# A transformer block with a mixture of experts: layer norm and gates after all tiles instead of tile by tile, and broadcast copies split over two engines

## What is computed

```python
x = x + layernorm(attention(layernorm(x)))
x = x + layernorm(ffn(layernorm(x)))

# ffn(y)
router = sigmoid(y @ gate_w + gate_b)                 # 16 values a token
values, idx = top_k(router, k=2); values /= sum(values)
out = y + mlp(y, shared) + sum(values * mlp(y, experts[idx]))
# mlp(y, wg, wu, wd) = (silu(y @ wg) * (y @ wu)) @ wd, 1024 -> 512 -> 1024
```

## Time and profile before

| what | us |
|---|---|
| two runs | 5123.9 and 5325.3, median 5224.6 |
| the profiled execution | 5133.07 |
| its span, slowest core (core 6) | 5131.5 |
| its eight cores | 5115.5 to 5131.5 |
| TensorE busy | 3719.8 (72%) |
| VectorE busy | 1558.9 (30%) |
| ScalarE busy | 856.7 (17%) |
| GpSimd busy | 125.4 (2%) |

### The profile page before, as it was taken

How to read it: one execution, slowest core, us unless ns; L and a number is a source line. 1 busy time by engine, 2 the same in 40 slices (tenths; PEclk the granted TensorE clock), 3 DMA queues, 4 the chain that set the end, 5 groups by cost and what they waited for, 6 DMA issues and landing times.

```text
span 5131.5 us, 69222 instructions; the slowest of 8 cores (5115.5 to 5131.5 us)
## 1 busy us (share of the span) xinstructions
PE 3719.8 (72%) x22032; PEld 2020.0 (39%) x22032; DVE 1558.9 (30%) x3716; ACT 856.7 (17%) x2069; POOL 125.4 (2%) x128
## 2 busy tenths in 40 slices
PE   0465454499579849948975984995698499479678
PEld 0232222255335425524542542553354255245445
DVE  0421002422432342243234234224323422432333
ACT  0210000211211221121112112112112111211111
POOL 0000000000000000000000000000000000000000
PEclk9777777799779969968986996997799699689889
DMA  9067777045225405513531550452254045135346
GB/s 181 1 119 160 171 169 192 1 164 210 70 85 215 144 17 188 191 49 116 212 117 42 209 188 6 164 210 70 76 216 152 17 177 194 58 115 205 120 149 229
DMA packets 137919, 688.80 MB, mean 134 GB/s; under 512 B 11744, under 2 KB 46560, under 8 KB 65776
## 3 DMA queue, kind: packets, MB, share of 16 engines
q1 hardware_dynamic: 89792, 621.96, 33.6%
q0 software_dynamic: 47792, 62.43, 8.2%
HBM read 676.51 MB, written 70.25 MB: 146 GB/s over the span
## 4 chain that ended last, share of the span: by engine, by line
PE 62%; DMA 10%; DVE 10%; issue 5%; DVEq 5%; ACT 4%; another core or an unknown queue 2%; POOL 1%; ACTq 0%; SPq 0%; POOLq 0%
PE PSA L834 17%; PE PSA L851 17%; PE PSA L893 16%; PE PSA L444 5%; DMA wu_sb<-ewu 5%; DVEq L89 5%; DMA wd_sb<-ewd 3%; DVE psb L537 2%; PE PSA L652 2%; PE PSA L474 2%; ACT psb L522 2%; DMA scru<-wu_sb 1%; DMA scrd<-wd_sb 1%; DVE ssum L529 1%
## 5 line engine op out<-in xcount | busy, mean ns | idle before, releaser
L834 PE MATMUL PSA<-z_fm,wg_sb 128*128 128x384 f16 (+1 forms) x5984 | 1044.4, 334 | 238.0 <-DMA wu_sb<-ewu 202.3
L862 DVE TENSOR_TENSOR us<-PSA,slabA 128x384 f16<-128x384 f32 (+1 forms) x704 | 384.3, 546 | 2291.6 <-PE PSA L851 2291.6
L893 PE MATMUL PSA<-wd_sb,hs 128*128 128x512 f16 x4352 | 992.3, 386 | 64.2 <-DMA wd_sb<-ewd 64.2
L851 PE MATMUL PSA<-z_fm,wu_sb 128*128 128x384 f16 (+1 forms) x5984 | 978.6, 321 | 2.7 <-DVE us L859 1.3
L834 PEld LDWEIGHTS PSA<-z_fm,wg_sb 128*128 128x128 f16 x5984 | 598.6, 101 | 674.7 <-issue 329.7
L851 PEld LDWEIGHTS PSA<-z_fm,wu_sb 128*128 128x128 f16 x5984 | 578.5, 98 | 374.5 <-issue 20.9
L839 ACT ACTIVATE gs<-PSA 128x384 f16<-128x384 f32 (+1 forms) x748 | 355.4, 480 | 2177.3 <-PE PSA L834 2176.8
L893 PEld LDWEIGHTS PSA<-wd_sb,hs 128*128 128x128 f16 x4352 | 430.7, 99 | 578.8 <-issue 101.5
L550 PE MATMUL PSA<-ids,psb 128*128 128x128 f16 x256 | 41.5, 297 | 350.1 <-DVE psb L537 350.1
L872 DVE TENSOR_TENSOR hs<-gs,us 128x384 f16<-128x384 f16 (+1 forms) x748 | 263.6, 352 | 63.1 <-issue 5.3
L410 PE MATMUL PSA<-ids,z_tm 128*128 128x128 f16 x256 | 29.3, 275 | 326.5 <-DVE z_fm L418 191.2
(11 more groups left out here) (91 smaller groups left out, 1759.7 us busy)
## 6 DMA issues: line engine op xcount, KB each, us to landing
wg_sb<-scrg SPq DMA_DIRECT2D x170, 1024.0 KB, 5.9
wu_sb<-scru SPq DMA_DIRECT2D x170, 1024.0 KB, 9.0
wd_sb<-scrd SPq DMA_DIRECT2D x170, 1024.0 KB, 6.9
scrg<-wg_sb SPq DMA_DIRECT2D x17, 1024.0 KB, 3.9
scru<-wu_sb SPq DMA_DIRECT2D x17, 1024.0 KB, 6.6
scrd<-wd_sb SPq DMA_DIRECT2D x17, 1024.0 KB, 4.5
wg_sb<-ewg POOLq DMA_DIRECT2D x16, 1024.0 KB, 11.5
wu_sb<-ewu POOLq DMA_DIRECT2D x16, 1024.0 KB, 15.8
```

Of the source, the lines that this page charges most:

```text
L834: last = e.matmul(PS[:, b, 0:ST], wg_sb[:, wb_i, kc, 128 * i:128 * i + 128], z1_fm[:, kc, 0:ST], start=(kc == 0), stop=(kc == 7))
L851: last = e.matmul(PS[:, b, 0:ST], wu_sb[:, wb_i, kc, 128 * i:128 * i + 128], z1_fm[:, kc, 0:ST], start=(kc == 0), stop=(kc == 7))
L862: em = k.emit("dve", lambda e, i=i, b=b, hp_=eidx % 2, eidx=eidx, ST=ST: e.tensor_tensor(out=us[:, hp_, i, 0:ST], in0=PS[:, b, 0:ST], in1= ...
L893: last = e.matmul(PS[:, bb, :], hs[:, hp_, i, 128 * tq:128 * tq + 128], wd_sb[:, wb_i, i, 512 * jh:512 * jh + 512], start=(first and i == ...
```

## The change

The three functions `emit_A8`, `emit_B1q` and `emit_gate` and the order written out above go. In their place stand three loops: first the output projection and residual of all tiles, then the second layer norm of all tiles with the helpers that the head uses too (all statistics and applies first, then all transposes and copies), then the gates of all tiles, each of which now waits for the copies of all tiles. The instructions are the same as before. The second edit is in the spreading of the router weights: of the 16 copies to wbc, those with an even number move from ScalarE to VectorE.

```diff
-        def emit_A8(q):
-            nonlocal prev_resadd
+        for q in range(NQ):
             bpair = (6, 7) if q % 2 == 0 else (2, 3)
...
-        def emit_B1q(q):
-            k.emit("dve", lambda e, q=q: e.bn_stats(bnst[:, 0, :], x_tm[:, q, 0:512]),
-                   waits=later(x2_mils[q]), drain_before=True)
...
-            y_evac_by_q[q] = evs
-
-        def emit_gate(q):
+        y_mils = ln_stats_apply(x_tm, z1_tm, x2_mils, 2)
+        yfm_mils, ytr_mils = transpose_tm_to_fm(z1_tm, z1_fm, y_mils, ret_tr=True)
+        yfm_all = later(yfm_mils[-1], *yfm_mils)
+
+        sig_mils = []
+        for q in range(NQ):
             b = 6 + q % 2
-            ws = later(*y_evac_by_q[q]) + bank_write_waits(b) + later(m_gw)
+            ws = yfm_all + bank_write_waits(b) + later(m_gw)
...
-        emit_A8(0)
-        if NQ > 1:
-            emit_A8(1)
-        emit_B1q(0)
-        if NQ > 2:
-            emit_A8(2)
-        if NQ > 1:
-            emit_B1q(1)
-        emit_gate(0)
-        if NQ > 2:
-            emit_B1q(2)
-        if NQ > 1:
-            emit_gate(1)
-        if NQ > 2:
-            emit_gate(2)
-        yfm_all = later(*yfm_mils)
...
-                    em = k.emit("act", lambda e, ei2=ei2, b=b, ST=ST: e.activation(
-                        out=wbc[:, ei2, 0:ST], in_=PS[:, b, 0:ST], func=AF.Identity,
-                        bias=0.0, scale=1.0), waits=later(pm), inc=True)
+                    if ei2 % 2 == 0:
+                        em = k.emit("dve", lambda e, ei2=ei2, b=b, ST=ST: e.tensor_copy(
+                            wbc[:, ei2, 0:ST], PS[:, b, 0:ST]), waits=later(pm), inc=True)
+                    else:
+                        em = k.emit("act", lambda e, ei2=ei2, b=b, ST=ST: e.activation(
+                            out=wbc[:, ei2, 0:ST], in_=PS[:, b, 0:ST], func=AF.Identity,
+                            bias=0.0, scale=1.0), waits=later(pm), inc=True)
```

More of the change, by code:

```diff
@@ L732, in emit_gate @@
-        def emit_gate(q):
+        if attn_only:
+            od = k.emit("sync", lambda e, T0=T0, NQ=NQ: e.dma_start(
+                out=outh[T0:T0 + 128 * NQ, :].rearrange("(q p) d -> p q d", p=128),
+                in_=x_tm[:, 0:NQ, :]), waits=later(*x2_mils), inc=("do", 16))
+            prev_x2_mils = x2_mils
+            prev_ytr = []
+            if sub_i + 1 < len(subs):
+                head_mils = emit_head(sub_i + 1)
+            continue
+        y_mils = ln_stats_apply(x_tm, z1_tm, x2_mils, 2)
@@ L754, in emit_gate @@
                         waits=later(t1), drain_before=True, inc=True)
-            sig_mils[q] = sg
-        emit_A8(0)
-        if NQ > 1:
-            emit_A8(1)
-        emit_B1q(0)
-        if NQ > 2:
-            emit_A8(2)
-        if NQ > 1:
-            emit_B1q(1)
-        emit_gate(0)
-        if NQ > 2:
-            emit_B1q(2)
-        if NQ > 1:
-            emit_gate(1)
-        if NQ > 2:
-            emit_gate(2)
-        yfm_all = later(*yfm_mils)
[L774 to L782, removed]
+            sig_mils.append(sg)
         wsb_mils = []
```

## The result

The changed kernel takes 5040.3 us (median of 11 executions, the lowest 5035.6); the kernel before took 5129.8 on the same footing (median of 10, the lowest 5123.9). The ratio is 0.983, with a 95% interval of 0.981 to 0.984. That is 89 us less where the prediction said 81; the time itself was forecast as 5052, within 5035 to 5070. Some executions of every kernel here run longer, with a lower granted clock on the cores of one die or both; ratios, and from here on times and stages, are those of the others.

What follows compares the result with a forecast made beforehand. A VectorE-centred chain was taken to bound the stretch before the experts, with TensorE waiting. The order's 85.9 us less 5 for the copies gave 81 us off 5133.1, so 5052 us, own range 5035 to 5070, wider range 5010 to 5135.

Steps and rivals of the forecast that it cites:

- The bound: Between attention and the first expert matmul, 46.5 us a block: a chain centred on VectorE sets the pace, TensorE waits.
- Tile 2's residual: Output projection: the third tile's residual follows the second's directly, at a pitch of 6.2 us, ending at 1437.76.
- The layer norms in a row: Second layer norm: three statistics at 2.76 us pitch, as at the kernel's start, then 3.76 us to the last copy.
- GpSimd beside VectorE: Second layer norm: GpSimd's apply beside VectorE's statistics costs nothing; if contention bit, 12 us of the gain would go.
- rival B: Layer norms don't overlap as at the start, through engine contention or queued transposes: 5064 to 5121 us, chance 0.12.
- What is late next: After the gates: first expert matmul 9.4 us earlier, 1.0 lost waiting for VectorE's top-2 block; a block gains 8.4.
- The copies: Router broadcast: half the copies on VectorE lengthen a bank's loop by 0.07 us, costing 0.5 us a block, 5 in all.
- rival A: Router broadcast: ScalarE's own time was the bound, so two engines gain 34 us; 5013 us, chance 0.10.
- rival C: Expert matmuls after TensorE's longer idling stay at the lower clock: no gain from 50 a block, 5213 us with 100; chance 0.08.
- The sum: Whole kernel: 85.9 us gained by the new order less 5 for the copies is 81 us, 1.6% less.
- part 1: New order tile by tile, up to the experts: 8.4 us in each of ten blocks, 1.9 in the eleventh, 85.9 in all.

Runs made afterwards that it cites:

- e4: Kernel before, third projection left in place, but all transposes, copies and gates moved behind all statistics; ratio 0.978 to the kernel before.
- e8: Changed kernel with the top-2 block done for all tiles at once, 10 VectorE instructions instead of 30; profiled execution 5026 us.
- e1: Changed kernel with all 16 broadcast copies back on ScalarE, so the new order alone; 5021 us.
- e2: Kernel before with only the second edit, half of the broadcast copies on VectorE; ratio 1.001 to the kernel before.
- e5: Changed kernel with the broadcast matmuls going round six banks instead of two, copies still alternating between VectorE and ScalarE; best execution 4975 us.
- e6: Changed kernel with six banks for the broadcast instead of two and all copies on ScalarE; ratio 0.973 to the kernel before.
- e7: Changed kernel with all 16 broadcast copies on VectorE and two banks; ratio 0.982 to the kernel before.
- e12: Changed kernel with six broadcast banks, copies on both engines, and the top-2 block for all tiles at once; ratio 0.975 to the kernel before.

## Why the prediction was right

**The bound.** A chain with VectorE at its centre set the stretch, and TensorE waited on it: shown by the stretch itself (22.9 us of VectorE in 46.5 us became 22.2 in 36.45) and by e4, where the same instructions in another order give 36.15.

**Tile 2's residual.** Foreseen: two residuals in 13.84 us after tile 0's; measured 1417.83 + 1.23 - 1405.45 = 13.61, and 13.41 on the mean of the middle blocks.

**The layer norms in a row.** Foreseen from the first block's head: 8.05 to the last nmr, then 3.76 to the last copy. Measured 1427.12 - 1419.06 = 8.06, then 1430.93 - 1427.12 = 3.81. The best step of the prediction was to find that the kernel already ran the new sequence once.

**GpSimd beside VectorE (rival B).** The 32 applies L388 take 1.184 to 1.195 us, as before, and the bn_stats L371 beside them 0.694 to 0.696. B is out. The Trainium skill (GPSIMD Engine Reference, its table of specifications) names contention only with VectorE instructions that have two SBUF inputs or run in a two-port mode. bn_stats has one input, and the trace agrees.

**What is late next.** Foreseen: 9.4 us gained up to the first expert matmul, 1.0 given back to VectorE's top-2 block. Measured over the middle blocks 10.06 and 0.89, and e8 took the 0.89 away by shortening that very block. Net that is 9.17 instead of 8.4. The largest part of the difference is the pitch of the residuals. I had 6.41 us for the second, as in the block that I read, and 6.2 for the third; over the middle blocks it is 6.1, before and after, so tile 2's residual ends 0.43 us earlier than I had it. Another 0.13 lies ahead of tile 0's residual (10.31 us from the first projection matmul instead of 10.44), where nothing was moved. The rest are tenths, 0.1 of them in what was given back.

**The copies.** This step was wrong, in its sign. I had a loss of 0.5 us a block, because TensorE takes the banks in turn and a bank with the longer copy would hold up both; measured is a gain of 0.2 (0.4 in the stretch, of which e1 has half without this edit). I had named 1.38 us for a pair; it is 1.28 to 1.31. VectorE lets TensorE go 0.14 us after its copy where I had carried over ScalarE's 0.26, which outweighs the copy's 0.07, so bank 6 goes round in 1.28 us. That keeps bank 6 from holding anything up, but the last matmul is bank 7's, whose copies stay on ScalarE at 1.31 us. There the gain is mostly in the first round: the first copy of bank 7 no longer stands behind bank 6's on ScalarE, and from the first matmul of bank 7 to its second it is 1.26 us in e2 where it was 1.38. In the whole time none of this can be told from nothing (e2). The reasoning behind the term, that a bank's round trip and no engine sets the pace of two banks, was right and is the most useful thing here (e5, e6, e7); rival A is out.

**The clock (rival C).** It showed, in small. Its sign came true in round 0: I had named more than some ten slow matmuls in L834, and over the middle blocks 13 to 14 of these 32 ran at the lower level where it had been 8 to 9. In the block above, the kernel before first, then the changed one:

```profile
1460.24:1467.78 7.54, 6.63 (x38) 3.46 (x35) 5.08 (x27) 2.88 (x6) 0.00 (x0) 0.83 0.00 0
...
1432.10:1439.76 7.66, 7.66 (x37) 3.90 (x35) 4.98 (x28) 3.19 (x6) 0.00 (x0) 0.67 0.00 0
```

The price was 0.12 us, since the slower matmuls only filled a wait for ScalarE that had stood among them:

```profile
1465.18 2.76 PE L834 MATMUL PSA<-z_fm,wg_sb 128*128 128x384 f16 x16 [0.91 <-ACT gs L839]
```

Behind the broadcast the first 32 matmuls of round 1 were slower too:

```profile
1486.64 7.09 PE L834 MATMUL PSA<-z_fm,wg_sb 128*128 128x384 f16 x32
...
1458.88 8.10 PE L769 MATMUL PSA<-z_fm,wg_sb 128*128 128x384 f16 x32
```

Over the middle blocks the stretch from there to the first L828 is 12.44 us for 12.16. So C costs 0.3 us a block there, not 8. (One reading under C was off: TensorE's idle time from 1423.12 on was 12.76 us, up to the transposes, not over 13.)

**The sum.** 81 us foreseen, 89 measured by the medians. The stages come to 94, which is what separates the two profiles: nine middle blocks with 9.3 us where 7.9 was foreseen (0.8 more in part 1, 0.9 in the broadcast, with the order's share, less 0.3 of the clock), the first block with 7.9, the last with 1.1 where 1.4 was foreseen, and 1.4 us ahead of the first block, where nothing was changed. That the first block gave just the 8.4 - 0.5 foreseen is luck, given how far its loads scatter. That leaves a total off by a tenth, with two errors that add up: tenths rounded against the change, and the copies.

## What to carry to other kernels

Where several engines take turns in short steps, look in each queue for a waiting instruction with ready work behind it: put all of one kind first, so that the tiles' waits lie under each other's work, and then ask which engine is late next and shorten that block. A short matmul with a copy on two PSUM banks is a round trip and not a load; more banks halved it, while a second copying engine gave 0.2 us on two banks and 1.0 on six (5.28 to 4.25), and only where the clock was up. So the banks come first, then the engine. Look in the profile for a place where the kernel already runs the new order: it prices the change better than any sum of single durations.

## What was not expected of the hardware

- The next matmul on a bank starts 0.14 us after VectorE's copy of it (e7), 0.26 after ScalarE's (the kernel before).
- ScalarE's copies of 128x384 from PSUM take 0.49 us in a row of the profile but start every 0.37 us when 16 are ready (e6), while their rows grow to 0.67. A sum of single durations overstates what ScalarE needs.
- The same 16 broadcast matmuls with copies on both engines took 5.16 us in e12 (granted clock 0.53) and 3.97 us in e5 (1.00 for the first 2.42 us, then 0.50). Twice a shorter top-2 block went with a lower clock in the broadcast behind it: 0.59 to 0.51 from the changed kernel to e8, 0.75 to 0.54 from e5 to e12.
